# Pre-LN scan and mixture-of-experts layer on one core: expert slots of 512 rows, with weights split where they were loaded

## The reference, cut to what matters

```python
x = x + attn(layernorm(x))          # x: (4, 1024, 256); rmsnorm, one projection to q, kv, a,
                                    # y[t] = sigmoid(a[t]) * y[t-1] + kv[t], result q * y
z = layernorm(x).reshape(4096, 256)
logits = z @ router_w.T             # 7 routed experts
top_vals, top_idx = top_k(logits, 2); top_w = softmax(top_vals)
def swiglu(z, wg, wu, wd):          # wg, wu: (256, 1024), wd: (1024, 256)
    return (silu(z @ wg) * (z @ wu)) @ wd
x = x + sum over the 2 chosen experts of top_w * swiglu(z, expert) + swiglu(z, shared expert)
```

## Time and profile before

| | |
|---|---|
| median of 3 runs | 1016.72 us (1016.47 to 1017.0) |
| the profiled execution's own time | 1016.68 us |
| its span, first to last instruction | 1014.9 us |
| TensorE busy | 98% |
| VectorE, ACT, GpSimd busy | 62%, 52%, 49% |
| DMA | 192.75 MB, mean 190 GB/s |

### The profile page before, as it was taken

One profiled execution on the slowest core, in us unless ns is written; L12 is line 12 of the kernel. 1 busy time (PEld: TensorE's weight loads), 2 busy tenths in 40 slices (PEclk: granted clock), 3 DMA queues, 4 the chain that ended last, 5 costly groups with the idle time before them and its releaser, 6 DMA issues.

```text
span 1014.9 us, 19709 instructions
## 1 busy us (share of the span) xinstructions
PE 998.5 (98%) x7277; PEld 941.3 (93%) x7277; DVE 629.3 (62%) x1095; ACT 523.5 (52%) x786; POOL 501.6 (49%) x282
## 2 busy tenths in 40 slices
PE   7999999999999999999999999999999999999998
PEld 6788999999999998999999999999999999999997
DVE  7997687887523365555555656565655555647876
ACT  4555433223222456666666667666666666643232
POOL 2226100000012469777777777778887777650000
PEclk9999999999999999999999999999999999999999
DMA  9333300000799748877777777777777777737441
GB/s 321 90 93 89 83 12 14 19 11 7 261 362 325 246 137 258 263 253 243 237 257 229 257 234 256 227 255 236 247 231 257 234 257 235 238 83 239 131 130 41
DMA packets 162029, 192.75 MB, mean 190 GB/s; under 512 B 76089, under 2 KB 147266, under 8 KB 151746
## 3 DMA queue, kind: packets, MB, share of 16 engines
q1 hardware_dynamic: 155248, 173.83, 53.3%
q0 software_dynamic: 6720, 18.36, 5.9%
q10 hardware_dynamic: 18, 0.01, 0.0%
HBM read 165.42 MB, written 26.74 MB: 189 GB/s over the span
## 4 chain that ended last, share of the span: by engine, by line
PE 88%; DVE 7%; ACT 1%; POOL 1%; DMA 1%; issue 1%; SPq 0%; DVEq 0%; POOLq 0%
PE ps L1020 51%; PE ps L1035 16%; PE ps L1039 8%; PE ps L1061 4%; PE ps L927 3%; PE ps L1069 2%; DVE y_sb L1209 2%; PE ps L911 1%; POOL w_both L594 1%; DVE hT_lo L1169 1%; ACT h_hi L797 1%; DVE h_lo L1539 1%; PE ps L938 1%; DVE h_early L1534 1%; DMA resid<-in_L_attn_x_dram 1%
## 5 line engine op out<-in xcount | busy, mean ns | idle before, releaser
L1020 PE MATMUL ps<-xs_hi,w_both 128*128 128x256 f32 x3072 | 564.7, 284 | 3.2 <-DVE ps L1534 2.4
L1020 PEld LDWEIGHTS ps<-xs_hi,w_both 128*128 128x128 f32 x3072 | 479.1, 189 | 6.0 <-DVE ps L1534 2.8
L1020 PE MATMUL ps<-xs_lo,w_both 128*128 128x256 f32 x1536 | 434.8, 283 | 0.0
L594 POOL TENSOR_TENSOR w_both<-raw,w_both 128x2048 fp32r<-128x2048 f32 x67 | 317.9, 4745 | 96.7 <-ACT w_both L753 88.4
L1020 PEld LDWEIGHTS ps<-xs_lo,w_both 128*128 128x128 f32 x1536 | 290.7, 189 | 0.1
L1035 PE MATMUL ps<-w_both,h_hi 128*128 128x512 f32 x768 | 273.5, 398 | 0.7 <-DVE h_lo L1539 0.6
L1039 PE MATMUL ps<-w_both,h_lo 128*128 128x256 f32 x768 | 215.5, 281 | 0.0
L792 ACT ACTIVATE silu<-ps 128x512 f32<-128x512 f32 x192 | 114.3, 595 | 190.5 <-PE ps L1020 190.5
L753 ACT ACTIVATE w_both<-raw 128x1024 fp32r<-128x1024 f32 x192 | 192.5, 1051 | 4.4 <-DMA raw<-in_L_ffn_w_gate_dram 2.5
L1534 DVE TENSOR_TENSOR ps<-ps,silu 128x512 f32<-128x512 f32 x160 | 111.8, 699 | 129.5 <-ACT silu L792 123.1
L1539 DVE TENSOR_TENSOR h_lo<-ps,h_hi 128x512 fp32r<-128x512 f32 x160 | 110.6, 691 | 107.8 <-ACT h_hi L797 107.8
(11 more groups left out here) (191 smaller groups left out, 741.0 us busy)
## 6 DMA issues: line engine op xcount, KB each, us to landing
raw<-in_L_ffn_w_up_dram SPq DMA_DIRECT2D x33, 1024.0 KB, 5.3
raw<-in_L_ffn_w_gate_dram SPq DMA_DIRECT2D x33, 1024.0 KB, 8.5
raw<-in_L_ffn_w_down_dram SPq DMA_DIRECT2D x33, 1024.0 KB, 5.6
sorted_rows<-x_stage SPq DMA_DIRECT2D x32, 256.0 KB, 2.2
x_rows<-sorted_rows SPq DMA_DIRECT2D x128, 64.0 KB, 5.3
got<-expert_rows SPq DMA_DIRECT2D x10, 512.0 KB, 5.7
z_rows<-z_all SPq DMA_DIRECT2D x8, 512.0 KB, 2.9
x_rows<-z_rows SPq DMA_DIRECT2D x64, 64.0 KB, 2.5
```

The costliest lines, as they stand in the source:

```text
L594: pool.tensor_tensor(w_lo[buf][:, k, :], source[:, k, :], w_hi[buf][:, k, :].bitcast(F32), ALU.subtract).then_inc(wlo_ready[k], 1)
L1020: last = pe.matmul(o, w[:, part, at[kd]:at[kd] + P], xx[:, u, kd, :], start=i == 0, stop=i == len(terms) - 1)
```

## The change

- **Quads.** Two slots of 256 rows become one of 512, a **quad**: 12 for the routed experts (QUADS), and for the shared expert `n` = 2, 4, 6, 8 and 12 and the last two. A quad counts as two slots in `n` and in all semaphores. Each of its gate/up matmuls has 512 columns, and a *unit* is now one hidden tile j (8 of them), gate in one bank and up in the next. Slots 0 and 1 stay as they are, and so do 8 routed slots of 256 rows (PAIRED), which follow the quads, and the 6 lones. A *turn* is one expert's use of loaded weights: 12 quads and 8 slots.
- **Down part of a quad.** Row tiles 0 and 1 as before in banks 4 and 5. Then tiles 2 and 3 in banks 6 and 7, tile by tile, each as one group of 512 columns. Bank 6 also takes the transposed rows, so TensorE first waits until the rows of the next two units are out of it. In the early quads both tiles share bank 6, and three matmuls of 256 columns stand for the pair of 512 and 256.
- **Weights split in place.** `raw` is gone. An expert's weights are loaded into the place of `w_lo` (`w_raw[b]`), rounded to `w_hi`, and overwritten by the remainder. Gate and up of turn r + 2 are loaded once the gate/up part of turn r is over, down of r + 1 once the down part of r - 1 is.
- **When weights are rounded.** ACT rounds for the next turn: in a quad the halves of up, gate and down in units 0 to 5; in a slot of 256 the halves of up and gate in pairs 0 to 3, and down after them. VectorE splits up in units 3 and 4 of a quad, or after the pairs of a slot; GpSimd splits gate and down as they come.
- **Rows** are transposed two units ahead (`turns`): in a quad the two halves of the next quad in units 1 and 4, in a slot those of n + 2.
- **Ranking** knows three kinds of place: fours (quads), pairs and singles; there are more small steps. The chunks of the lists are made in quads 2, 4 and 6.
- **Mixing.** SBN = 4. ACT multiplies by the weight (`weigh`, two instructions a row tile), VectorE adds the two products and then adds them to the rows (`mix`), several row tiles at once.

```diff
+            def load_gate_up(r, b, ahead, sources=None):
+                sources = sources or rows_of_expert(r + NS)
+                sp.wait_ge(gu_psum, ahead * PAIRS)
+                for k in (1, 0):
+                    sp.dma_start(parts_of(w_raw[b])[k], sources[k]).then_inc(raw_in[b][k], 16)
+            with sp.Fori(0, QUADS // 2) as i:
+                for u in range(2):
+                    load_down(i * 2 + (u + 1), 1 - u, i * 4 + (R0 + 2 * u))
+                    for par in range(2):
+                        put_and_load(i * 4 + (2 * u + 4 + par), par, i * 2 + (u + 2))
+                    load_gate_up(i * 2 + (u + 2), u, i * 4 + (R0 + 2 * u + 2))
+            for j in range(PAIRED):
+                r, n, u = QUADS + j, R0 + 2 * QUADS + j, j % 2
+                load_down(r + 1, 1 - u, n, shared_rows if r + 1 == TURNS else None)
+                v = n + 4 - R0
+                if v < ROUTED:
+                    put_and_load(v, u, v // 2)
+                else:
+                    load_x(n + 4, SA + v - ROUTED, z_dram, u)
+                if r + 2 <= TURNS:
+                    load_gate_up(r + 2, u, n + 1, shared_rows if r + 2 == TURNS else None)
...
 GpSimd
+            for r in range(QUADS):
+                i = NS + 2 * r
+                gather_ahead(i + 4)
+                split_lo(0, r + 2, 1 - r % 2)
+                gather_ahead(i + 5)
+                split_lo(2, r + 2, 1 - r % 2)
+                scatter_y(i)
+                scatter_y(i + 1)
+            for r in range(QUADS, TURNS):
+                i = NS + QUADS + r
+                if i + 4 < NS + ROUTED:
+                    gather_ahead(i + 4)
+                split_lo(0, r + 2, 1 - r % 2)
+                split_lo(2, r + 2, 1 - r % 2)
+                scatter_y(i)
...
 ACT, slot(n, h, r=None, nxt=None, turns=(), ...)
-                    if p < 2 and down is not None:
-                        round_w(2, 1 - u, down, p)
-                    if p == PAIRS - 2 and not last:
-                        x_hi(n + 1, 1 - u)
+                    if nxt is not None:
+                        round_w((1, 1, 0, 0)[p], nxt[0], nxt[1], p % 2)
+                    for at, ahead in turns:
+                        if at == p:
+                            x_hi(n + ahead, (h + ahead) % 4)
...
-                if gate_up is not None:
-                    for k in (1, 0):
-                        for half in range(2):
-                            round_w(k, u, gate_up, half)
+                if nxt is not None:
+                    for half in range(2):
+                        round_w(2, nxt[0], nxt[1], half)
...
+            def quad(n, h, r=None, nxt=None, turns=((2, 2), (5, 3)), early=False, between=()):
+                for j in range(JH):
+                    q = n * PAIRS + j
+                    par = j % 2
+                    act.wait_ge(gu_psum, q + 1)
+                    act.activation(silu[:, par, :, :], ps[:, 2 * par, :]..., ACT.Silu).then_inc(silu_ready, 1)
+                    act.wait_ge(gated, q + 3)
+                    if j == 0:
+                        act.wait_ge(down_psum, n + 1)
+                    act.activation(h_hi[:, j, :]..., h32_of(par, early), ACT.Copy).then_inc(hhi_ready, 1)
+                    if nxt is not None and j < 6:
+                        round_w((1, 1, 0, 0, 2, 2)[j], nxt[0], nxt[1], j % 2)
+                    for at, ahead in turns:
+                        if at == j:
+                            x_hi(n + ahead, (h + ahead) % 4)
+                    if j in between:
+                        between[j]()
...
 TensorE
+            def quad(n, h, buf, m=None, between=(), skip=NS, ahead=2, early=False):
+                pe.wait_ge(x_split, n - skip + 2)
+                if m is not None:
+                    for k in range(2):
+                        pe.wait_ge(wlo_ready[k], m + 1)
+                for j in range(JH):
+                    pe.wait_ge(gated, n * PAIRS + (j + 1))
+                    if j in between:
+                        between[j]()
+                    for part in range(2):
+                        ...
+                            last = pe.matmul(ps[:, 2 * (j % 2) + part, :],
+                                             w[:, part, kd * H + j * P:kd * H + (j + 1) * P],
+                                             xx[:, h // 2, kd, :], start=i == 0, stop=i == len(terms) - 1)
+                    last.then_inc(gu_psum, 1)
...
+                if JH in between:
+                    between[JH]()
+                if ahead:
+                    pe.wait_ge(x_split, n - skip + 4)
+                for t in range(ST, 2 * ST):
+                    for j in range(JH):
+                        if not early:
+                            last = down_wide(j, both, hi, (t,))
+                            continue
...
 VectorE
+            def quad(n, h, turns=(), kind="pair", nxt=None, routed=None, shared=None, early=False, ...):
+                for j in range(JH):
+                    gate(n, j, par, early, skip, ...)
+                    rest(n, j, par, early, skip, ...)
+                    if j in between:
+                        between[j]()
+                    for at, ahead, nth in turns:
+                        if j == at + 1 and kind == "pair":
+                            x_lo(n + ahead - skip + 1, (h + ahead) % 4)
+                    for at, ahead, nth in turns:
+                        if j == at:
+                            turn(n, h, ahead, nth, skip, kind)
+                    if nxt is not None and j in (3, 4):
+                        split_half(*nxt, j - 3)
...
+            betweens = {
+                2: {0: lone_targets, 2: find_pairs, 3: find_over, 4: move_pairs, 5: move_alone,
+                    6: move_over, 7: move_on, "down": rows_of_first, "half": first_lists},
+                4: {0: lambda: hot_rows(1), 3: lambda: hot_cols(1), 6: lambda: hot_rows(2), 7: lambda: hot_cols(2),
+                    "down": lambda: lists(3), "half": lambda: lists(4)},
+                6: {1: lambda: hot_rows(5), 3: lambda: hot_cols(5), 6: lambda: hot_rows(6), 7: lambda: hot_cols(6),
+                    "down": lambda: lists(7), "half": last_lists}}
...
+            with dve.Fori(0, QUADS // 2) as i:
+                for u in range(2):
+                    nth = i * (2 * LD) + loads(R0 + 2 * u + 2)
+                    quad(i * 4 + (R0 + 2 * u), 2 - 2 * u, turns=((1, 2, nth), (4, 3, nth)),
+                         nxt=(i * 2 + (u + 2), 1 - u), routed=i * 4 + (2 * u + 1))
```

More of the change, by code:

```diff
@@ L845, in _ @@
-            slot(NB0 - 2, 0, r=NS + ROUTED - 1, down=16 * ROUTED, gate_up=16 * ROUTED + 16)
-            slot(NB0 - 1, 1, r=NS + ROUTED, down=16 * ROUTED + 16)
-            with act.Fori(0, SBN // 2 - 1) as i:
-                for u in range(2):
-                    slot(i * 2 + (NB0 + u), u)
-            slot(NB0 + SBN - 2, 0)
-            slot(NB0 + SBN - 1, 1, last=True)
+            quad(LATE, LATE % 4, turns=())
+            lone(2, between={p: lambda p=p: round_w((1, 1, 0, 0)[p], 0, loads_of(0, 0), p % 2) for p in range(4)})
@@ L1044, in slot, with down_wide @@
                 last.then_inc(down_psum, 1)
+            def down_wide(j, both, hi, tiles=range(ST)):
+                for t in tiles:
+                    pe.matmul(ps[:, 4 + t, :].rearrange("p (b d) -> p b d", d=D),
+                              h_hi[:, j, t * P:(t + 1) * P], both[:, :, 2, j * D:(j + 1) * D],
+                              start=j == 0, stop=False)
+                    last = pe.matmul(ps[:, 4 + t, 0:D], h_lo[:, j, t * P:(t + 1) * P],
+                                     hi[:, 2, j * D:(j + 1) * D], start=False, stop=j == JH - 1)
+                return last
@@ L1521, in split_half, with loads, add_wide @@
                 if half:
[L1522 to L1524 removed]
+                    ins.then_inc(wlo_ready[1], 1)
+            def loads(n):
+                return LD * (n // 2 + 1)
+            added = [0]
+            def add_wide(n, tile, bank=4):
+                rows = resid[:, tile:tile + ST, :]
+                dve.wait_ge(down_psum, n + 2)
+                if tile >= T0:
+                    dve.wait_ge(mixed, MIX_FROM[tile // ST - SA] + ST)
+                added[0] += 1
+                dve.tensor_tensor(rows, ps[:, bank:bank + 2, 0:D], rows, ALU.add).then_inc(half_added, 1)
+                dve.wait_ge(half_added, added[0])
+                dve.tensor_tensor(rows, ps[:, bank:bank + 2, D:2 * D], rows, ALU.add).then_inc(down_free, 1)
+                dve.wait_ge(down_free, n + 2)
@@ new lines, in _ @@
+            for n in range(2, FIRST_LONE - 2, 2):
+                quad(n, n % 4, turns=ahead_of(n), shared=n, early=True, skip=0, between=betweens[n])
+            n = FIRST_LONE - 2
+            quad(n, n % 4, turns=ahead_of(n), kind="lone", shared=n, skip=0)
+            for i in range(2):
+                lone(i)
+            quad(LATE, LATE % 4, turns=ahead_of(LATE), kind="lone", shared=SA - 2, skip=2)
+            lone(2)
```

(1 more changed line is left out.)

821 lines of the change are left out of this document (437 added, 384 removed).

## The result

The changed kernel takes **1114.26 us** (median of 4 runs, 1113.86 to 1115.43), the kernel before 1016.86 on the same chip: a ratio of 1.0959, 95% interval 1.0940 to 1.0978. Forecast was slower, 1069 us, with a range up to 1088. The direction was right, and 45 us are missing from the sum.

What follows compares the result with a forecast made beforehand. TensorE, busy 98% of the span, was taken to bound the kernel. Terms +9.4, +24.7, +6.8, -2.7, +6.4, -2.6 and +10.6 gave +52.6: span 1014.9 to 1067.5, plus 1.8 for the ends, 1069 us; range 1042 to 1088.

Steps and rivals of the forecast that it cites:

- The wide matmul: Gate/up part of a quad: 512-column matmuls at 227 ns, so a quad that never waits takes 33.04 us against 34.32.
- Start of the routed part: First routed turn: its weights are prepared well ahead in the lone slots, so two stalls of today go, -2.7 us.
- early quads: Quads 2, 4 and 6 and slot 1: list and ranking work delays VectorE, +6.4 us together.
- the wait for the lists: Quad 6: TensorE stands between its down halves until list chunk 7 is made, 3.5 to 4 us.
- The chain in the quads, 35.1: Twelve routed quads: the serial ACT and VectorE work delays gate 5 and stalls TensorE; 35.1 us each, +9.4 in all.
- the two halves of a weight split take 2.36, one 1.2: VectorE in routed quads: price of a weight split half, 1.2 us, used in the gate periods of units 3 and 4.
- The eight slots, 20.25, by GpSimd's subtraction: Slots of 256: the next slot waits for GpSimd's w_lo of gate; 3.1 us a slot, +24.7 for eight hand-overs.
- the ring: First four slots of 256: next rows move before weights on SP's queue, 21.95 us instead of 20.25, +6.8 for four.
- The clock, 0.08: Rival, chance 0.08: after the eight slot gaps of 3 us TensorE runs at 1.2 GHz, +23 us, 1092 us.
- The last two quads, 36.5 and 42.7: Mixing at the end: weighing on ACT at 0.5 us each and VectorE's adds lengthen both quads, +10.6 us against 68.6.

Runs made afterwards that it cites:

- GpSimd waiting: Changed kernel with one more wait: in the routed quads GpSimd's gate subtraction starts only after VectorE's two halves of the up weights; 1083.64 us, ratio 1.0645.
- where the gap is filled: Changed kernel with 38 transposes of the identity on TensorE at the start of each slot of 256, before its wait for the weights; 1103.62 us, ratio 1.0857.
- two other runs: Changed kernel with quads untouched: one with the slots' gate weights first (1067.39 us), one with only ScalarE's order in the slots changed (1100.97 us).

## Why the prediction was wrong, point by point

TensorE waits at the places that the forecast named, in the quads behind gate 5 and at each slot's start, and two steps of its sum failed: VectorE's half of a weight split was priced at 1.2 us wherever it stands, and it measured 3.0 to 5.6 us beside GpSimd's subtraction; and the fall of the clock behind the waits stood in the sum with nothing. The first costs 16.6 us in the quads and about 6 in the slots, the second 27.

- **The wide matmul** (227 ns, a quad without waits 33.04): right, 33.08. (A slip beside it: 1824 times 2.5 ns are 4.6 us, not 4.7. No term of the sum uses it.)
- **Start of the routed part, early quads**: right; 393.06 against 393.6. Quads 2, 4 and 6 took 37.25, 35.6 and 41.6 (38.3, 35.8, 40.4), the wait for the lists was 2.8 us (3.5 to 4), and the clock fell behind it, which I had not priced; quad 6 took 40.12 in two later runs in which it did not fall.
- **The chain in the quads, 35.1**: the mechanism and the size were right for the work that I listed. With VectorE's halves at the 1.2 us that I took for them, in their units, a quad takes 35.0 (GpSimd waiting), and with the chain's order changed 33.4. The step that failed is "the two halves of a weight split take 2.36, one 1.2". In the row that I took it from, VectorE's pair ended at 513.92 and GpSimd's subtraction began at 513.51: they hardly met. I read a duration without asking what ran beside it, and the change moves both into the same 5 us. It costs 12 x (36.48 - 35.1) = 16.6 us in the quads before any clock. The Trainium skill ("SBUF — State Buffer", SBUF: two separate sides) has the rule that I didn't bring in: a VectorE instruction with two inputs in SBUF and a GpSimd instruction that reads SBUF take the same ports by an exclusive lock; the one that starts first has them for its whole length, and the other blocks. The trace agrees: 1.22 us issued first, 2.97 when issued inside GpSimd's 5.28, ending 1.08 us behind it.
- **The eight slots, 20.25, by GpSimd's subtraction**: the hand-over is a wait, as worked out, and in the first slot, which no fall of the clock precedes, GpSimd's subtraction begins at 15.44 (15.3 forecast) and ends at 20.65 (20.1). But TensorE goes on at 21.98, not at 20.25: the same failed step once more, since VectorE's second half stands until GpSimd is through. The forecast had no wait for VectorE in a slot at all. Without the clock a slot costs 21.88 - 17.16 = 4.7 more than before, 37.8 in all; with the ring I had 31.5.
- **The ring of rows and weights on SP's queue, 21.95 (+6.8)**: not seen. The slots that have it, the first four, are no longer than the others, best seen where the gap is filled and the clock stays at 1.00: 21.84 to 21.93 against 21.84 to 21.95. At this length it doesn't bind; whether it would at 20.25 with SP's old order no run tested. With SP's order changed, slots of 18.07 run.
- **The clock, 0.08**: this rival was right in kind and came on top of the forecast. I had rows for 1.5 us of idle time only, and the forecast itself contained eight gaps of 3 us, so it should have had a far greater chance; and the range ended at 1088, below the 1092 that I gave it, though it was said to take in most of this case. Price: 12.9 us in the slots (1.8 behind each of seven gaps, where I had taken 2.9), and 10 x 1.43 = 14.3 in the quads, where I had expected none. 27 of the 45 us are the clock's, but it follows from the waits: with a wait of 0.76 or 1.0 us in the quads it fell in none.
- **The last two quads, 36.5 and 42.7**: 35.9 and, without the tail's 4.2 us, 39.45. The second is short because a weighing takes 0.40 us in a row of many (24 in 9.70) and four between two links take 1.70, not the 0.5 each that I took from a group of four; ScalarE is through in time, and the first silu is not held for 2 us.

```profile
1061.61 9.70 ACT L902 ACTIVATE got<-got,mix_w 128x256 f32<-128x256 f32 x24
1071.81 0.60 ACT L844 ACTIVATE silu<-ps 128x512 f32<-128x512 f32 x1 [0.50 <-PE ps L1125]
```

- **Sum of the misses**: quads 16.6 + 14.3, slots 6.2 + 12.9, last two -3.8, start -0.5: 45.7, and 45.0 were measured between the two spans.

Shown by experiments: the meeting of the two subtractions, its price in the quads, the clock's price in the slots, the order in the slots. Worked out from traces alone: the clock's price in the quads, from ten quads against two, with the same difference in the 24 quads of two other runs.

## What to carry to other kernels

A duration belongs to what ran beside it: before a row prices a moved instruction, look at the other engines in that row's microseconds and in those where it will go, above all for VectorE and GpSimd both reading SBUF. Where a sum contains new waits of TensorE longer than any in its rows, it has to hold a price for the clock too. And in a chain that several engines share, what is queued between two links counts more than the sum of the work: moving roundings, transposes, split and loads, with no instruction less, took 52 us off, some 30 of them by ending the meeting of the two subtractions.

## What the runs showed of the hardware that I had not expected

- The two engines take turns by instruction. With only ScalarE's order changed, VectorE's two halves against GpSimd's two subtractions take 3.02 and 5.51 us and GpSimd's second 5.50, each half ending about 1.1 us behind GpSimd's; alone they take 1.22 and 4.6. VectorE's `tensor_tensor` with one operand in PSUM isn't held up (0.69 us inside GpSimd's 5.28).
- The granted clock fell to 0.5 for 3.4 us behind waits of 2.5 us in most quads, but not in all (10 of 12; 9 and 8 of 12 in the two other runs), and for 3.4 or 6.8 us behind gaps of 4.6. Behind quad 6's wait of 2.8 it fell in some runs and not in others. Behind waits of 1.8 to 1.9 us it fell at three places, counted over all runs; behind waits of 1.5 us and less it never did.
- Transposes on TensorE held the granted clock at 1.00 across seven gaps behind which it had fallen: 38 of them, 4.3 us, in each slot of 256.
